# Attention and channel-mixing kernel: reordered opening, spread x loads, a shorter row stage with a Sigmoid gate, inverse-root chains cut in three

## The chip, the core and the metric

The kernel runs on one core of one Trainium2 chip. The metric is the device time of one execution in microseconds (us). An execution is also profiled: every instruction's start and duration on the five engines TensorE (PE), VectorE (DVE), ScalarE (ACT), GpSimd (POOL) and SyncE (SP, which issues DMAs).

## The reference

```python
x = x + _layernorm(_L0_attn_ref(_layernorm(x), weight))     # x: 4 x 1024 x 128
x = x + _layernorm(_L0_ffn_ref(_layernorm(x), W_r, W_k, W_v, mu_r, mu_k))
# attention, 16 heads of 8 channels, queries = keys = y, values = the whole y
scores = einsum('bhtk,bhsk->bhts', y, y) / sqrt(8)
o = einsum('bhts,bsc->bhtc', softmax(scores), y)            # then o @ weight, 2048 -> 128
# channel mixing; x_prev is x shifted by one position
r = sigmoid((mu_r * x + (1 - mu_r) * x_prev) @ W_r.T)
k = (mu_k * x + (1 - mu_k) * x_prev) @ W_k.T
out = r * (square(relu(k)) @ W_v.T)
```

## The kernel before

The work is cut into 4 batches of 1024 positions, 8 rows of 512 queries, 128 steps (row, head) and 256 quads; a quad is four key blocks of 128 against 512 queries, so a step is two quads. One loop over k runs on every engine, each engine in its own written order, with semaphores between them.

For quad k, `score(k)` writes four banks of `ps_s` on TensorE; it waits until the exponential of quad k-1 has read them. `weigh(k)` on ACT takes the exponential into `e_f` (float32). `cast(k)` on POOL issues a DMA that rounds `e_f` to the float16 `e_hi`. `split_quad` on DVE, written in iteration k+2, computes `e_lo = e_f - e_hi`. `products(k)`, written in iteration k+4 (`LAG`), multiplies y_hi by e_hi, y_hi by e_lo and y_lo by e_hi: twelve matmuls of 512 columns. After two quads `take_o` (ACT), `split_o` (DVE), `project` (TensorE), `invert` (DVE), `scale` (ACT) and `add` (DVE) normalize a head's result, apply its slice of the weight and add it to `acc`. SP loads the operands `op_s` and `op_t` four steps ahead (`OP_RING`).

When the 16 heads of row r are added, its row stage runs beside the next row's quads. `rows_at(k)` gives its offset o = k - (32 (r+1) + 8), from 0 to `SPAN` - 1, and each engine's `row_part(o, r)` says what it does at which offset: centre and statistics, an inverse root, normalize, add x, statistics, an inverse root, transpose, mix with the shifted row, key, gate and value matmuls, gating, statistics, an inverse root, normalize, add. `inv_root` (line 271) is a chain of 7 or 9 tiny POOL instructions, each waiting for the one before, in the same POOL queue as the casts. `next_batch(k)` does the same for the preparation of the next batch: statistics, root, normalize, split, squares, transposes, and a shift bound `shx` that DVE computes and TensorE transposes (`turn_shift`). The gate is computed as 1 / (1 + exp(-g)): exponential on ACT (line 569), add (781) and four reciprocals (785) on DVE. The row stage, the batch preparation and the opening share one PSUM bank, `ps_x`.

Ahead of the loop stands the opening: the first batch is loaded, normalized, split, transposed and written to DRAM scratch, the attention weight is scaled, centred (`weights_less`, `weights_centred`) and split into w_hi and w_lo. SP issues the x loads of batches 1 to 3 in one block (line 229).

## Time and profile before

| | |
|---|---|
| median of 3 runs (lowest, highest) | 1064.0 us (1063.06, 1066.88) |
| the profiled execution, its own time | 1063.41 us |
| its span, first to last instruction | 1061.6 us |
| mean granted TensorE clock | 0.954 |
| busy: PE, DVE, ACT, POOL | 88%, 85%, 69%, 28% |
| DMA engines, time of cast packets (q0) | 65.3% of the span |
| first and last exponential of the loop | 36.68 us, 996.33 us |

Busy shares are of the whole span. An engine that is idle gets the name of whatever released it; that name is the last link of a chain and need not be its cause. The granted clock is 1.0 at 2.4 GHz and 0.5 at 1.2 GHz.

### The profile page before, as it was taken

To read this page: it belongs to the slowest core of one execution; us is meant where nothing else is said; L and a number is where in the kernel's file an instruction comes from. 1 tells how busy PE (TensorE), PEld (TensorE's weight loads), DVE (VectorE), ACT (ScalarE), POOL (GpSimd) and SP (SyncE) were. 2 spreads that over 40 slices of the span, in tenths; PEclk is the share of its full clock that TensorE was granted. 3 is DMA by queue.
4 is the path that set the end of the run, shared out by engine and by line. 5 is a ranking of instruction groups with operands and counts; after the bars stand their busy time and mean duration, and the time that the engine had idled before them with its cause. 6 is when DMAs were issued, how large, how long until landed. Compare 5 with 4: busy or idle time off the path is not lost.

```text
span 1061.6 us, 17583 instructions
## 1 busy us (share of the span) xinstructions
PE 929.4 (88%) x5930; PEld 442.6 (42%) x5930; DVE 900.7 (85%) x1163; ACT 730.5 (69%) x1007; POOL 302.3 (28%) x521
## 2 busy tenths in 40 slices
PE   1659999989998899989998889988999899989922
PEld 1224444444544345434444335444444345444411
DVE  6658899889897899969988899969989689979953
ACT  1537777868777677867777667876787677777621
POOL 2101431123115541243115541153113341154021
PEclk9879999999999999989999999998999999999965
DMA  5689899998886788888987788886988788878700
GB/s 166 130 178 183 166 186 185 192 206 181 178 180 138 164 171 170 180 198 176 187 172 146 146 178 173 180 203 151 201 167 175 154 177 180 179 144 170 141 10 10
DMA packets 100344, 174.41 MB, mean 164 GB/s; under 512 B 21536, under 2 KB 62880, under 8 KB 100256
## 3 DMA queue, kind: packets, MB, share of 16 engines
q0 software_dynamic: 36864, 134.23, 65.3%
q1 hardware_dynamic: 63392, 39.06, 13.5%
q8 instruction: 48, 0.79, 0.3%
q14 instruction: 40, 0.33, 0.1%
HBM read 28.51 MB, written 10.49 MB: 37 GB/s over the span
## 4 chain that ended last, share of the span: by engine, by line
PE 37%; DVE 19%; issue 17%; POOL 13%; DMA 7%; ACT 5%; SPq 1%; DVEq 0%; POOLq 0%; ACTq 0%
PE ps_o L426 10%; POOL fnw L277 9%; PE ps_o L427 9%; PE ps_o L428 9%; DVE e_lo L703 8%; DMA e_hi<-e_f 6%; PE ps_s L411 3%; ACT e_f L524 3%; POOL nw L277 2%; POOL e_hi L314 2%; ACT part L536 2%; DVE eg L785 2%; DVE fst L730 1%; DVE o_neg L709 1%; PE ps_r L439 1%
## 5 line engine op out<-in xcount | busy, mean ns | idle before, releaser
L703 DVE TENSOR_TENSOR e_lo<-e_f,e_hi 128x2048 f16<-128x2048 f32 x256 | 590.9, 2308 | 85.9 <-DMA e_hi<-e_f 85.6
L524 ACT ACTIVATE e_f<-ps_s 128x2048 f32<-128x2048 f32 x256 | 482.0, 1883 | 181.1 <-PE ps_s L411 171.4
L426 PE MATMUL ps_o<-e_hi,y_hi 128*128 128x512 f16 x1024 | 397.4, 388 | 29.9 <-DVE o_neg L709 26.5
L428 PE MATMUL ps_o<-e_hi,y_lo 128*128 128x512 f16 x1024 | 395.3, 386 | 0.0
L427 PE MATMUL ps_o<-e_lo,y_hi 128*128 128x512 f16 x1024 | 395.2, 386 | 0.0
L314 POOL DMA_DIRECT2D e_hi<-e_f x256 | 138.2, 540 | 682.3 <-ACT e_f L524 645.7
L536 ACT ACTIVATE part<-ps_r,rden 128x128 f32<-128x128 f32 x512 | 145.8, 371 | 72.7 <-DVE rden L715 72.7
L426 PEld LDWEIGHTS ps_o<-e_hi,y_hi 128*128 128x128 f16 x1024 | 100.9, 99 | 183.6 <-issue 82.3
L428 PEld LDWEIGHTS ps_o<-e_hi,y_lo 128*128 128x128 f16 x1024 | 101.6, 99 | 125.3 <-issue 7.8
L427 PEld LDWEIGHTS ps_o<-e_lo,y_hi 128*128 128x128 f16 x1024 | 101.6, 99 | 95.1 <-issue 7.4
L411 PE MATMUL ps_s<-op_t,op_s 32*128 32x512 f16 x1024 | 102.1, 388 | 35.9 <-ACT e_f L524 25.0
L725 DVE TENSOR_TENSOR acc<-acc,part 128x512 f32<-128x512 f32 x120 | 81.6, 680 | 21.5 <-ACT part L536 21.5
L439 PE MATMUL ps_r<-w_hi,o_hi 128*128 128x128 f16 x512 | 93.0, 220 | 1.2 <-ACT part L536 1.2
L440 PE MATMUL ps_r<-w_lo,o_hi 128*128 128x128 f16 x512 | 92.9, 220 | 0.0
L441 PE MATMUL ps_r<-w_neg,o_neg 128*128 128x128 f16 x512 | 92.7, 220 | 0.0
L709 DVE SCALAR_TENSOR_TENSOR o_neg<-o_hi,ps_o 128x512 f16<-128x512 f16 x128 | 86.2, 673 | 6.9 <-ACT o_hi L529 4.8
L529 ACT ACTIVATE o_hi<-ps_o 128x512 f16<-128x512 f32 x128 | 77.7, 607 | 1.7 <-PE ps_o L428 1.7
L411 PEld LDWEIGHTS ps_s<-op_t,op_s 32*128 32x128 f16 x1024 | 26.1, 91 | 104.8 <-issue 69.4
L439 PEld LDWEIGHTS ps_r<-w_hi,o_hi 128*128 128x128 f16 x512 | 50.5, 99 | 16.9 <-issue 2.4
L440 PEld LDWEIGHTS ps_r<-w_lo,o_hi 128*128 128x128 f16 x512 | 50.4, 98 | 15.6 <-issue 1.1
L277 POOL TENSOR_TENSOR fnw<-fnw,consts 128x4 f32<-128x4 f32 x88 | 53.0, 603 | 6.9
L441 PEld LDWEIGHTS ps_r<-w_neg,o_neg 128*128 128x128 f16 x512 | 50.3, 98 | 0.0
(122 smaller groups left out, 467.1 us busy)
## 6 DMA issues: line engine op xcount, KB each, us to landing
e_hi<-e_f POOLq DMA_DIRECT2D x256, 512.0 KB, 4.9
op_t<-scr_t SPq DMA_DIRECT2D x512, 32.0 KB, 3.4
op_s<-scr_s SPq DMA_DIRECT2D x512, 16.0 KB, 3.1
scr_s<-yT SPq DMA_DIRECT2D x12, 256.0 KB, 4.5
scr_t<-yT SPq DMA_DIRECT2D x12, 256.0 KB, 3.8
xs<-in_L_attn_x_dram SPq DMA_DIRECT2D x4, 512.0 KB, 9.3
out_dram<-res SPq DMA_DIRECT2D x8, 256.0 KB, 2.2
scr_s<-eighth SPq DMA_DIRECT2D x4, 256.0 KB, 3.2
```

What stands on the lines that cost most here:

```text
L277: nc.gpsimd.tensor_tensor(out, in0, in1, op).then_inc(s, 1)
L314: nc.gpsimd.dma_start(flat(e_hi[:, ring]), flat(e_f[:, k % EF_RING])).then_inc(cast_in[ring], 16)
L411: mm = nc.tensor.matmul(ps_s[:, g, :], op_s[here, slot, q * P:(q + 1) * P], op_t[here, slot, :], start=True, stop=True)
L426: nc.tensor.matmul(dst, y_hi[:, b % 2, s, :], e_hi[:, ring, g, :], start=(q == 0 and g == 0), stop=False)
L427: nc.tensor.matmul(dst, y_hi[:, b % 2, s, :], e_lo[:, ring, g, :], start=False, stop=False)
L428: mm = nc.tensor.matmul(dst, y_lo[:, b % 2, s, :], e_hi[:, ring, g, :], start=False, stop=(q == 1 and g == 3))
L439: nc.tensor.matmul(dst, o_hi[:, j % 2, here], w_hi[:, j % H, :], start=True, stop=False)
L440: nc.tensor.matmul(dst, o_hi[:, j % 2, here], w_lo[:, j % H, :], start=False, stop=False)
L441: mm = nc.tensor.matmul(dst, o_neg[:, j % 2, here], w_neg[:, j % H, :], start=False, stop=True)
L524: nc.scalar.activation(e_f[:, k % EF_RING], ps_s[:], ACT.Exp, scale=1.0 / ROOT).then_inc(weighed, 1)
L536: ins = nc.scalar.activation(part[:, j % 2, i, :], ps_r[:, i * P:(i + 1) * P], ACT.Identity, scale=rden[:, j % 2, i:i + 1])
L703: dve.tensor_tensor(flat(e_lo[:, ring]), flat(e_f[:, k % EF_RING]), flat(e_hi[:, ring]), ALU.subtract).then_inc(split, 1)
```

## The change

**Root chains.** `inv_root` gets a part number: two steps, three steps, two or four steps. The three parts of a chain are written in three successive iterations, behind that iteration's cast. A batch's squares go from POOL to ACT.

**Row stage.** `SPAN` is 41. Offsets before and now: centre, sums, moments 3, 4, 5 to 1, 2, 3; root 7 to 4-6; normalize (ACT) 9 to 7; add x, sums, moments 11, 12, 13 to 9, 10, 11; root 15 to 12-14; z 17 to 16; transposes (PE) 19 to 17; copy (ACT) 20 to 18; mixes 22, 23 to 20, 21, the gate's first; gate matmul 26 to 22; key matmul still 24; value matmul still 28; gating 34 to 30; root 38 to 33-35; normalize 40 to 36; last add 42 to 38. The gate is a Sigmoid on ACT at offset 23, and the key matmul waits for it; add and reciprocals are gone. For the last row ACT has a Sigmoid of one column at offset 8.

**x loads.** One each at quads 6, 20 and 34, after that quad's scores.

**Opening.** The first root is computed on DVE. One Newton round of two goes from the shift bound, and `turn_shift` comes two iterations later. The maximum of w_raw and the weight's centring follow the shift on DVE, over the whole weight at once; the matmuls with `less` stand between the first four scores, and ACT and DVE split the weight a quarter per iteration. The four `op_t` loads of step 0 are issued by ACT, the four `op_s` loads by SP.

```diff
+                    sp.dma_start(*op_s_load(j, g)).then_inc(op_in[slot], 16)
+                    if j > 0:
+                        sp.dma_start(*op_t_load(j, g)).then_inc(op_in[slot], 16)
...
-            for b in range(1, B):
-                sp.dma_start(xs[:, b * NB:(b + 1) * NB, :], x_v[:, b]).then_inc(x_in[b], 16)
             for k in range(LAST):
+                if k in (6, 20, 34):
+                    b = (6, 20, 34).index(k) + 1
+                    sp.wait_ge(scored, k)
+                    sp.dma_start(xs[:, b * NB:(b + 1) * NB, :], x_v[:, b]).then_inc(x_in[b], 16)
...
+            def inv_root(part_, s, before, v, y, a, var, n, eps=consts[:, 0:1], bias=None, mean=None):
+                three_halves, minus_half, minus_one = (consts[:, i:i + 1].to_broadcast([P, n]) for i in (1, 2, 3))
+                steps = [before + (0, 2, 5)[part_]]
...
+                    pool.wait_ge(s, steps[0])
+
+                if part_ == 0:
+                    go(v, var, eps.to_broadcast([P, n]), ALU.add)
+                    go(y, v, minus_half, ALU.pow)
+                if part_ == 1:
+                    go(a, y, y, ALU.mult)
+                    go(a, a, v, ALU.mult)
+                    go(a, a, minus_half, ALU.mult)
+                if part_ == 2:
+                    go(a, a, three_halves, ALU.add)
+                    go(y, y, a, ALU.mult)
+                    if bias is not None:
+                        go(bias, mean, y, ALU.mult)
+                        go(bias, bias, minus_one, ALU.mult)
...
-                if o == 7:
-                    root_row(0, r)
-                if o == 15:
-                    root_row(1, r)
-                if o == 17:
-                    ge(pool, mix_r, r)
+                for i, first in enumerate((4, 12, 33)):
+                    if 0 <= o - first < 3:
+                        root_row(i, r, o - first)
+                if o == 14:
+                    ge(pool, mix_k, r)
...
-                if o == 38:
-                    root_row(2, r)
...
-                    if o == 20:
-                        root_batch(b)
-                    if o == 26:
-                        square_batch(b)
+                    if 19 <= o < 22:
+                        root_batch(b, o - 19)
...
+                pe.wait_ge(w_centred, 1)
...
+                    if j < 2:
+                        pe.wait_ge(w_split, j + 1)
...
-                if o == 19:
+                if o == 17:
                     pe.wait_ge(z_ok, r + 1)
...
-                if o == 24:
-                    pe.wait_ge(mix_k, r + 1)
-                    ge(pe, kv_ps, r)
-                    nc.tensor.matmul(ps_x[:], wT[:, 1, :], mix[:, 1, :], start=True, stop=True).then_inc(key_ps, 1)
-                if o == 26:
+                if o == 22:
                     pe.wait_ge(mix_r, r + 1)
-                    pe.wait_ge(key_relu, r + 1)
                     for i in range(RB):
                         mm = nc.tensor.matmul(ps_x[:, i * P:(i + 1) * P], mix[:, 0, i * P:(i + 1) * P], wT[:, 0, :],
                                               start=True, stop=True)
                     mm.then_inc(gate_ps, 1)
...
+                if o == 24:
+                    pe.wait_ge(mix_k, r + 1)
+                    pe.wait_ge(gate_ok, r + 1)
+                    nc.tensor.matmul(ps_x[:], wT[:, 1, :], mix[:, 1, :], start=True, stop=True).then_inc(key_ps, 1)
                 if o == 28:
                     pe.wait_ge(key_ok, r + 1)
-                    pe.wait_ge(gate_exp, r + 1)
...
-            weight_top()
-            pe.wait_ge(w_in, 16)
-            for i in range(3):
-                weights_less(i)
-            pe.wait_ge(w_centred, 1)
-            weights_less(3)
             for k in range(LAST):
                 if k < QUADS:
                     score(k)
+                if k == 0:
+                    weight_top()
+                if k < 4:
+                    weights_less(k)
...
+            def weights_high(i):
+                act.wait_ge(w_scale, 2)
+                act.wait_ge(w_less, i + 1)
...
+                act.wait_ge(normed, b + 1)
+                nc.scalar.activation(flat(sq[:]), flat(yn[:]), ACT.Square).then_inc(squared, 1)
...
-                if o in (9, 40):
-                    i, src, dst, done_ = (0, acc[:, r % 2], xn, a_normed) if o == 9 else (2, gated, res, f_normed)
+                if o in (7, 36):
...
-                if o == 20:
+                if o == 8 and r == ROWS - 1:
+                    nc.scalar.activation(idle[:], consts[:, 0:1], ACT.Sigmoid)
+                if o == 18:
...
+                if o == 23:
+                    act.wait_ge(gate_ps, r + 1)
+                    ge(act, f_gated, r)
+                    nc.scalar.activation(flat(gate[:]), ps_x[:], ACT.Sigmoid).then_inc(gate_ok, 1)
...
-                if o == 27:
-                    act.wait_ge(gate_ps, r + 1)
-                    ge(act, f_gated, r)
-                    nc.scalar.activation(flat(eg[:]), ps_x[:], ACT.Exp, scale=-1.0).then_inc(gate_exp, 1)
...
+            act.wait_ge(scr_in[0], 7 * 16)
+            for g in range(4):
+                act.dma_start(*op_t_load(0, g)).then_inc(op_in[0], 16)
...
+            def batch_root():
+                v, y, a = (nw[:, i, :] for i in range(3))
+                c = nr[:, 0, 0:NB]
+                step(dve.tensor_scalar(v, mv[:, :, 1], EPS, None, ALU.add))
+                step(dve.tensor_scalar(a.bitcast(I32), v.bitcast(I32), 1, None, ALU.logical_shift_right))
+                step(dve.tensor_scalar(y.bitcast(I32), a.bitcast(I32), -1.0, float(MAGIC), ALU.mult, ALU.add))
+                for _ in range(3):
+                    step(dve.scalar_tensor_tensor(out=a, in0=y, scalar=-0.5, in1=y, op0=ALU.mult, op1=ALU.mult))
+                    step(dve.tensor_tensor(c, a, v, ALU.mult))
+                    step(dve.scalar_tensor_tensor(out=y, in0=c, scalar=1.5, in1=y, op0=ALU.add, op1=ALU.mult))
+
...
+            def batch_sqrt(b):
+                v, y, a, c = (nr[:, i, :] for i in range(4))
+                step(dve.scalar_tensor_tensor(out=a, in0=y, scalar=-0.5, in1=y, op0=ALU.mult, op1=ALU.mult))
+                step(dve.tensor_tensor(c, a, v, ALU.mult))
+                step(dve.scalar_tensor_tensor(out=y, in0=c, scalar=1.5, in1=y, op0=ALU.add, op1=ALU.mult))
...
-                v, y, a, c = (nr[:, i, :] for i in range(4))
-                for _ in range(2):
-                    step(dve.scalar_tensor_tensor(out=a, in0=y, scalar=-0.5, in1=y, op0=ALU.mult, op1=ALU.mult))
-                    step(dve.tensor_tensor(c, a, v, ALU.mult))
-                    step(dve.scalar_tensor_tensor(out=y, in0=c, scalar=1.5, in1=y, op0=ALU.add, op1=ALU.mult))
...
+                dve.wait_ge(w_in, 16)
+                dve.tensor_reduce(w_max[:, 0:1], w_raw[:], AX.XY, ALU.max)
...
+                step(dve.tensor_reduce(w_mean[:], w_raw[:], AX.X, ALU.add))
+                step(dve.tensor_scalar(w_mean[:], w_mean[:], 1.0 / C, None, ALU.mult))
+                dve.tensor_tensor(w_raw[:], w_raw[:], w_mean[:].unsqueeze(2).to_broadcast([P, H, C]),
+                                  ALU.subtract).then_inc(w_centred, 1)
...
+                dve.wait_ge(w_high, i + 1)
...
-                if o == 3:
+                if o == 1:
...
-                if o == 17:
+                if o == 16:
...
-                if o == 22:
+                if o == 20:
...
-                if o == 29:
-                    dve.wait_ge(gate_exp, r + 1)
-                    dve.tensor_scalar(eg[:], eg[:], 1.0, None, ALU.add).then_inc(gate_one, 1)
-                if 30 <= o < 34:
-                    i = o - 30
-                    dve.wait_ge(gate_one, r + 1)
-                    dve.reciprocal(eg[:, i, :], eg[:, i, :]).then_inc(gate_ok, 1)
-                if o == 34:
+                if o == 30:
                     dve.wait_ge(kv_ps, r + 1)
-                    dve.wait_ge(gate_ok, RB * (r + 1))
-                    dve.tensor_tensor(flat(gated[:]), flat(eg[:]), ps_x[:], ALU.mult).then_inc(f_gated, 1)
-                if o == 35:
+                    dve.wait_ge(gate_ok, r + 1)
+                    dve.tensor_tensor(flat(gated[:]), flat(gate[:]), ps_x[:], ALU.mult).then_inc(f_gated, 1)
...
-                if o == 42:
+                if o == 38:
...
+            dve.wait_ge(moment, 1)
+            batch_root()
             batch_normalize(0, range(NB))
             batch_split(0)
+            batch_squares(0)
...
-            dve.tensor_tensor(flat(sq[:]), flat(yn[:]), flat(yn[:]), ALU.mult).then_inc(squared, 1)
-            dve.wait_ge(w_in, 16)
-            dve.tensor_reduce(w_max[:, 0:1], w_raw[:], AX.XY, ALU.max)
...
-            batch_squares(0)
```

What the edit of the row stage does to POOL's queue, at the first row's first root (`fnw` is the root's scratch, `e_hi<-e_f` a cast). Before:

```order
35 L314 DMA e_hi<-e_f 128x2048 x19
36 L277 TENSOR_TENSOR fnw<-fmv,ws 128x4
37 L277 TENSOR_TENSOR fnw<-fnw,consts 128x4
38 L277 TENSOR_TENSOR fnw<-fnw 128x4 x2
39 L277 TENSOR_TENSOR fnw<-fnw,consts 128x4 x2
40 L277 TENSOR_TENSOR fnw<-fnw 128x4
41 L277 TENSOR_TENSOR fnw<-fmv,fnw 128x4
42 L277 TENSOR_TENSOR fnw<-fnw,consts 128x4
```

POOL's queue at the same place of the changed program:

```order
33 L326 DMA e_hi<-e_f 128x2048 x16
34 L291 TENSOR_TENSOR fnw<-fmv,ws 128x4
35 L291 TENSOR_TENSOR fnw<-fnw,consts 128x4
36 L326 DMA e_hi<-e_f 128x2048
37 L291 TENSOR_TENSOR fnw<-fnw 128x4 x2
38 L291 TENSOR_TENSOR fnw<-fnw,consts 128x4
39 L326 DMA e_hi<-e_f 128x2048
40 L291 TENSOR_TENSOR fnw<-fnw,consts 128x4
41 L291 TENSOR_TENSOR fnw<-fnw 128x4
42 L291 TENSOR_TENSOR fnw<-fmv,fnw 128x4
43 L291 TENSOR_TENSOR fnw<-fnw,consts 128x4
44 L326 DMA e_hi<-e_f 128x2048
```

Nine steps in one block have become two, three and four, with a cast between.

On ACT, at the gate of the first row (`eg` is the gate's exponential, `kr` the key). Before:

```order
133 L565 ACTIVATE kr<-kr 128x512
134 L524 ACTIVATE e_f<-ps_s 128x2048
135 L536 ACTIVATE part<-ps_r,rden 128x128 x4
136 L569 ACTIVATE eg<-ps_x 128x512
137 L524 ACTIVATE e_f<-ps_s 128x2048
```

ACT at the gate of the changed program:

```order
134 L549 ACTIVATE part<-ps_r,rden 128x128 x4
135 L585 ACT_TABLE_LOAD
136 L585 ACTIVATE gate<-ps_x 128x512
137 L537 ACT_TABLE_LOAD
138 L537 ACTIVATE e_f<-ps_s 128x2048
139 L542 ACTIVATE o_hi<-ps_o 128x512
```

The compiler has put a table load ahead of the Sigmoid and another ahead of the next exponential. There are seven of the first kind (rows 0 to 6; the eighth gate needs none) and six of the second, besides the one at the program's start.

On TensorE, at the end of the opening (`ps_s<-op_t,op_s` are scores, `w_raw,less` the weight). Before:

```order
6 L387 MATMUL ps_x<-ident,shx 128x128 x8
7 L392 MATMUL ps_r<-ident,w_max 1x128
8 L394 MATMUL ps_r<-w_top,ones 128x1
9 L399 MATMUL ps_o<-w_raw,less 128x512 x2
10 L399 MATMUL ps_r<-w_raw,less 128x512
11 L399 MATMUL ps_o<-w_raw,less 128x512
12 L411 MATMUL ps_s<-op_t,op_s 128x512 x20
```

TensorE at the end of the changed opening:

```order
6 L400 MATMUL ps_x<-ident,shx 128x128 x8
7 L426 MATMUL ps_s<-op_t,op_s 128x512 x4
8 L405 MATMUL ps_r<-ident,w_max 1x128
9 L407 MATMUL ps_r<-w_top,ones 128x1
10 L415 MATMUL ps_o<-w_raw,less 128x512
11 L426 MATMUL ps_s<-op_t,op_s 128x512 x4
```

The first scores stand ahead of the weight's matmuls, which follow one per quad.

## Rows read from the trace of the kernel before

**Rows 1.** The page, part 1: busy us of each engine (share) xinstructions

```profile
PE 929.4 (88%) x5930; PEld 442.6 (42%) x5930; DVE 900.7 (85%) x1163; ACT 730.5 (69%) x1007; POOL 302.3 (28%) x521
```

**Rows 2.** Timeline of ACT, 261 to 281: start, us, engine, line, names

```profile
265.27 1.88 ACT L524 ACTIVATE e_f<-ps_s 128x2048 f32<-128x2048 f32 x1
...
270.74 1.14 ACT L536 ACTIVATE part<-ps_r,rden 128x128 f32<-128x128 f32 x4
271.99 1.88 ACT L524 ACTIVATE e_f<-ps_s 128x2048 f32<-128x2048 f32 x1
...
276.60 1.88 ACT L524 ACTIVATE e_f<-ps_s 128x2048 f32<-128x2048 f32 x1 [2.24 <-PE ps_s L411]
```

**Rows 3.** Timeline of ACT: first exponential, that of quad 8, the last

```profile
36.68 1.88 ACT L524 ACTIVATE e_f<-ps_s 128x2048 f32<-128x2048 f32 x1 [9.03 <-PE ps_s L411]
...
71.56 1.88 ACT L524 ACTIVATE e_f<-ps_s 128x2048 f32<-128x2048 f32 x1 [12.38 <-PE ps_s L411]
...
996.33 1.88 ACT L524 ACTIVATE e_f<-ps_s 128x2048 f32<-128x2048 f32 x1 [0.96 <-PE ps_s L411]
```

**Rows 4.** Waits of PE, 36.7 to 1010: us in total, times, longest

```profile
PE ps_o L426 <- DVE o_neg L709: 26.5, 19, 4.8
PE ps_s L411 <- ACT e_f L524: 25.0, 15, 3.2
PE ps_s L411 <- DMA op_t<-scr_t: 10.9, 1, 10.9
PE ps_x L387 <- DVE shx L661: 3.6, 2, 3.0
PE ps_o L426 <- DVE e_lo L703: 3.2, 2, 1.7
```

**Rows 5.** Windows, PE: window, us, busy (x), granted clock, DMA share, GB/s

```profile
157.50:996.30 838.80, 791.16 (x5130) 0.98 0.85 175
```

**Rows 6.** Timeline of POOL, 318 to 352: the third root of row 0

```profile
325.40 1.51 POOL L277 TENSOR_TENSOR fnw<-fmv,consts 128x4 f32<-128x4 f32 x1
326.99 1.03 POOL L277 TENSOR_TENSOR fnw<-fnw,consts 128x4 f32<-128x4 f32 x1
...
330.52 3.11 POOL L277 TENSOR_TENSOR fnw<-fnw,consts 128x4 f32<-128x4 f32 x2
...
334.83 0.61 POOL L314 DMA_DIRECT2D e_hi<-e_f  x1 [0.36 <-POOL fnw L277]
```

**Rows 7.** The page, parts 5 (busy, mean ns) and 6 (KB, us to landing)

```profile
L703 DVE TENSOR_TENSOR e_lo<-e_f,e_hi 128x2048 f16<-128x2048 f32 x256 | 590.9, 2308 | 85.9 <-DMA e_hi<-e_f 85.6
...
L314 POOL DMA_DIRECT2D e_hi<-e_f x256 | 138.2, 540 | 682.3 <-ACT e_f L524 645.7
...
e_hi<-e_f POOLq DMA_DIRECT2D x256, 512.0 KB, 4.9
```

**Rows 8.** Timeline of the opening

```profile
15.90 2.28 DVE L807 TENSOR_REDUCE w_max<-w_raw 128x1 f32<-128x2048 f32 x1
...
30.20 0.33 SPq L217 DMA_DIRECT2D op_s<-scr_s  x1
...
33.69 0.43 SPq L219 DMA_DIRECT2D op_t<-scr_t  x1
```

**Rows 9.** Groups by line, ACT: busy us, mean ns, idle before

```profile
L572 ACT ACT_TABLE_LOAD x1 | 1.3, 1283 | 0.7 <-PEq L862 0.7
```

**Rows 10.** The chain that ended last, from 1003: start, us, what

```profile
1018.22 0.69 DVE acc L725
...
1022.29 0.59 DVE fsum L749
...
1040.13 0.70 DVE mix L772
...
1041.66 2.09 PE ps_x L455 x2
...
1047.70 3.40 DVE eg L785 x4
```

More of the change, by code:

```diff
@@ L108, in sandwich @@
         xn = sb("xn", [P, RB, C], F32)
+        idle = sb("idle", [P, 1], F32)
         x1 = sb("x1", [P, RB, C], F32)
@@ L113, in sandwich @@
         kr = sb("kr", [P, BANK], F32)
-        eg = sb("eg", [P, RB, C], F32)
+        gate = sb("gate", [P, RB, C], F32)
         gated = sb("gated", [P, RB, C], F32)
@@ L396, in weights_less @@
             def weights_less(i):
+                pe.wait_ge(w_centred, 1)
                 if i == 2:
                     pe.wait_ge(w_scale, 1)
-                mm = nc.tensor.matmul((ps_o[:, 0, :], ps_o[:, 1, :], ps_r[:])[i % 3], less[:],
-                                      flat(w_raw[:, 4 * i:4 * i + 4, :]), start=True, stop=True)
-                mm.then_inc(w_less, 1)
+                if i == 3:
+                    pe.wait_ge(shift_ready, 1)
+                nc.tensor.matmul(weights_ps(i), less[:], flat(w_raw[:, 4 * i:4 * i + 4, :]), start=True,
+                                 stop=True).then_inc(w_less, 1)
             def score(k):
```

145 lines of the change are left out of this document (71 added, 74 removed).

## The prediction

> **What bounds the kernel now.** I read the page first: TensorE (PE) is busy 88% of the span, VectorE (DVE) 85% [rows 1]. Two engines so close to full do not say which one sets the time, so I looked for the beat of the loop. Undisturbed, a pair of quads takes 271.99 - 265.27 = 6.72 us from exponential to exponential [rows 2]. TensorE has no idle time in that beat: one score group, twelve 512-column products, and every second quad a projection. 255 intervals at 3.36 us would be 857 us. The first exponential starts at 36.68 and the last at 996.33 [rows 3], so the loop takes 959.7 us, about 102 us more than its beat. That 102 us, the 36.7 us ahead of it and the 65.2 us behind it (1061.6 - 996.33) are what a change can win.
>
> Where do the 102 us go? Next the waits of TensorE inside the loop [rows 4]: 26.5 us for o_neg, 25.0 for e_f (about 8 of them before the fifth quad, where the pipeline fills), 10.9 once for an operand DMA, 3.6 for shx, 3.2 for e_lo. Without the filling and the DMA that is 26.5 + 17 + 3.6 + 3.2 = 50 us. Then the clock: from quad 32 to the last exponential, 838.8 us, the granted clock is 0.98 of full [rows 5]; 0.02 x 838.8 = 17 us, partly inside the waits. What is left is TensorE's own work for the row stage and the batch preparation, which nothing here removes.
>
> What starts those 50 us? The engines that TensorE waits for are not the cause: DVE and ScalarE (ACT) are late because a cast is late. POOL issues the cast DMA of each quad, and the same in-order queue runs the inverse-root chains. One chain of nine small steps stood in front of a cast from 325.40 to 334.83 [rows 6]: 9.4 us between two casts that are 3.36 apart in the beat. The steps themselves are 0.2 us, the pow 1.03; the long ones (two steps in 3.11) stood still beside a running e_lo. ACT waited for the end of that chain as well, and with it the next exponential. How much delay is free? Products stand four quads behind their scores, 13.4 us. Exponential 1.88, cast issue 0.54, transfer 4.9, split 2.31 [rows 3, 7] are 9.6: some 3.8 us to spare. So a 9 us hold shows on TensorE and a 3 us hold hardly does.
>
> **The change part by part.**
>
> *Root chains in pieces.* A chain of nine steps becomes two, three and four steps with a cast behind each. By [rows 6] the first piece is 326.99 + 1.03 - 325.40 = 2.6 us, the others some 2.5 to 4 us when they meet a running e_lo subtraction. A quad has 3.36 us, less 0.54 for the cast, so each cast is late by 0 to 1.5 us, inside the margin of 3.8. Squaring a batch leaves POOL (three times) and goes to ACT, where 1024 columns take about half of the 1.88 us that 2048 take [rows 3], in a long quad: hidden. The shift is issued two quads later on TensorE, which removes the 3.6 us wait for shx. Of the 50 us I let 12 stay: two quads carry a piece of two chains at once, and ACT's two normalizations now follow the last piece by one quad. Term -38, bounds -25 (half stays) and -46. With the waits go the drops of the clock behind them: of the 17 us in [rows 5] I take -12 (bounds -5, -15).
>
> The Trainium skill (SBUF — State Buffer, terms, shared port pair) says that DVE and GpSimd lock one port pair for a whole instruction and that the loser blocks fully. The stretched steps of [rows 6] agree with it. By that rule cutting the chain shortens no step, and every piece can lose a whole subtraction: the term would be the -25 of the first rival, not -38.
>
> *x loads spread.* Three loads of x stood in one block behind the first operand loads, and TensorE waited 10.9 us for an operand [rows 4]; the exponential of quad 8 began at 71.56 [rows 3]. Now one load each is issued at quads 6, 20 and 34, each ahead of operands that are needed six quads later (20 us). That returns the 10.9 and, since TensorE comes out of such a stand at the lower clock, an estimated 2.5 more; each load still takes DMA time from the casts: +1 each. Term -10.4, bounds -4 and -13.
>
> *Opening.* The first root moves from POOL (pow 1.03 as in [rows 6] among its seven steps) to DVE (twelve short ones): an estimated -0.9. The w_max reduction (2.28 [rows 8]) and the squaring leave DVE's path, y_lo moves behind two reductions and becomes the last input: net -0.8. One Newton round fewer: -1.0. The eight operand loads of the first step were issued one by one from 30.20 to 33.69 [rows 8]; now four on SP and four on ACT's queue side by side: -1.9. First exponential about 4.6 us earlier, at 32. The weight preparation, which stood before it, now stands between the first scores on TensorE and ACT, with two full-width DVE passes over w_raw ahead of the second quad: it gives back about 2.5 by quad 8. Term -2.1, bounds +2 and -5.
>
> *Sigmoid gate.* Per row this takes an add (0.4 us) and four reciprocals (3.4 us [rows 10]) off DVE; the beat hides them now (no wait of TensorE lies there), so they count nothing in the loop except as slack. It puts a table load before the Sigmoid and another before the next exponential, six times in the loop. Before has one load only, at the very start, 1.28 us [rows 9]. In the quad concerned, the exponential follows the four scalings at once (270.74 + 1.14, then 271.99 [rows 2]). Inserting 1.28 + 0.62 + 1.28 starts it 3.1 us late, at 275.1; it ends at 277.0. TensorE has products, projection and the key matmul in that quad; the exponential after it began at 276.60 [rows 2], its score 0.45 earlier, at 276.15. So TensorE waits 0.9. I take 1.3 with hand-offs. Term +8; bounds +5 and, if nothing covers the 3.2, +19.
>
> The Trainium skill (ScalarE: Activation LUTs, What ACT_TABLE_LOAD costs) has 1.28 us for the load and a drain of about 1.38 with each switch. The row agrees on the first; no row of before shows a drain. By that figure a pair costs 2.8 us more, the wait is 3.7, and the term would be +22: this speaks against the change.
>
> *Tail.* The last sum of the last row ends at 1018.91, but its centring starts at 1022.2 [rows 10], because reciprocals, gating and statistics of row 6 stand between. With row 6 finished earlier in quads: -3.3. POOL did row 6's chain ahead of row 7's; it now starts sooner, against the DVE work of row 7, and about 1.2 less of it lies on the path: -1.3. Row 7's own gate: before, 11.0 us from mix_d (1040.13) to the end of the reciprocals (1047.70 + 3.40) [rows 10], gate exponential and add included, the value product hidden beside them. Now the order is mix_r, gate product, Sigmoid 0.6, key product 2.09 [rows 10], relu and square 1.2, value product, each product about as long as the key's: 10.1 with two mixes and hand-offs. -0.9. Term -5.5, bounds -3 and -7.
>
> *Sum* against this execution (span 1061.6, 1063.4 with what lies around it, 0.6 under the median of 1064.0): -38 - 12 - 10.4 - 2.1 + 8 - 5.5 = -60. 1063.4 - 60 = 1003.4; with the offset to the median **1004 us**.
>
> **The rivals.**
> - *The casts stay late.* The steps still stand still behind e_lo, pieces run to 4 or 5 us, and six pieces follow one another at the end of each row. For it: 3.11 us for two steps [rows 6]. Against: the margin of 3.8 us. Half of waits and clock stay: 25 + 8 us in place of 12 + 5, about +17, and 3 more for the thinner distances: 1024.
> - *Switching the table costs more than its row.* If ACT stands twice as long, each of the six is 3.6: +14, 1018.
> - *A x load stalls again* in mid-loop, where DMA is as busy as it was at quad 7. Two of three at half the old price: +11, 1015.
> - *Slower.* POOL's first piece stands one quad behind DVE's moments, where it stood two. If DVE runs late there, POOL waits for it with the next cast queued behind, DVE then waits for that cast, and the lateness feeds itself. There are 21 chains in the loop; at 60 / 21 = 2.9 us each the whole gain is gone. For it: DVE is 85% busy. Against: DVE loses 3.8 us of work per row, and in [rows 4] no wait begins at the moments. 1065 to 1080.
> - *The change does nothing:* the waits have another cause than the chains; only opening, x loads, tail and tables count: 1063 - 18 + 8 = 1053.
>
> **How the numbers follow.** Forecast 0.60 (own range 988 to 1014), casts late 0.17, table 0.10, x load 0.06, nothing 0.03, slower 0.03, the rest 0.01 about unchanged. The low end adds the favourable bounds of the two largest terms (-8, -3) and some of the opening (-5): 986. The high end takes in the late casts with a dearer table: 1030. Range 986 to 1030. A measurement of this kernel tells about 0.5% from no change, some 5 us. Faster by more: 0.95; within: 0.02; slower: 0.03.
>
> **What would show it.** First exponential near 32, that of quad 8 near 58. TensorE's waits for o_neg and e_f in the loop at about 12 us together past the filling; clock 0.99 or more there. No POOL hold above 4.5 us between casts. Seven row gates with one table load each and six loads in front of exponentials, each pair with a TensorE wait of 1 to 1.5 us behind it. From the last sum to the end 37 us in place of 42.7. Wrong if the o_neg waits stay above 15 us (pieces do not free the casts), or if the exponential behind a Sigmoid begins over 4 us late.

## The result: 1006 us, and the profile after

| | before | after |
|---|---|---|
| time, median (range), us | 1065.44 (1063.06 to 1067.48, 4 runs) | 1006.24 (1004.64 to 1009.22, 4 runs) |
| ratio to before, 95% interval | | 0.9448 (0.9413 to 0.9484) |
| profiled execution: span, us | 1061.6 | 1007.4 |
| granted clock, mean | 0.954 | 0.978 |
| first exponential, last one, end of span, us | 36.68, 996.33, 1061.6 | 31.79, 948.77, 1007.4 |

The forecast was 1004. In the two profiled executions the 54.2 us come off at three places: 4.9 ahead of the first exponential, 42.7 in the loop (959.7 to 917.0), 6.6 behind it (65.2 to 58.6). What follows in this section is the changed kernel. The page, part 1, beside [rows 1]:

```profile
PE 913.3 (91%) x5930; PEld 437.1 (43%) x5930; DVE 867.4 (86%) x1112; ACT 750.8 (75%) x1028; POOL 327.2 (32%) x513
```

Timeline of ACT, the exponentials of [rows 3]:

```profile
31.79 1.88 ACT L537 ACTIVATE e_f<-ps_s 128x2048 f32<-128x2048 f32 x1 [6.42 <-PE ps_s L426]
...
56.00 1.88 ACT L537 ACTIVATE e_f<-ps_s 128x2048 f32<-128x2048 f32 x1 [1.15 <-PE ps_s L426]
...
948.77 1.88 ACT L537 ACTIVATE e_f<-ps_s 128x2048 f32<-128x2048 f32 x1 [2.27 <-PE ps_s L426]
```

Waits of PE from 36 to 960 (total, times, longest), and the windows of the loop (busy of PE, PEld, DVE, ACT, POOL, then granted clock, DMA share, GB/s):

```profile
PE ps_s L426 <- ACT e_f L537: 16.0, 17, 2.2
PE ps_o L443 <- DVE o_neg L753: 11.2, 14, 1.4
PE ps_s L426 <- DMA op_t<-scr_t: 2.1, 1, 2.1
PE ps_x L395 <- DVE diag L683: 2.0, 2, 1.0
PE ps_x L467 <- DVE z L785: 1.3, 1, 1.3
```

```profile
31.80:138.80 107.00, 101.71 (x620) 45.12 (x620) 93.83 (x105) 81.92 (x99) 27.25 (x40) 1.00 0.95 194
138.80:948.70 809.90, 780.91 (x5138) 373.81 (x5137) 726.90 (x890) 643.60 (x879) 285.56 (x418) 1.00 0.89 182
```

The reader is to see three things. The 10.9 us DMA wait of [rows 4] has become 2.1. The o_neg wait is less than half, its longest case 1.4 in place of 4.8. But o_neg and e_f together are still 27 us, spread over 31 waits of about 1 us. Of these, 1.9 us are the filling of the pipeline (8.1 before), so 25 us stand against the 12 that were predicted, and 29 with diag and z. The granted clock is 1.00 in both windows, where [rows 5] had 0.98.

Why 25 are left shows on POOL. Row 0's third root, that of [rows 6], now ends at 298.33, and the first root of row 1 follows in the next quads. Timeline of POOL, this first root of row 1, between two casts each time:

```profile
298.69 0.58 POOL L326 DMA_DIRECT2D e_hi<-e_f  x1 [0.36 <-POOL fnw L291]
299.29 2.27 POOL L291 TENSOR_TENSOR fnw<-fmv,ws 128x4 f32<-128x4 f32 x1
301.64 1.04 POOL L291 TENSOR_TENSOR fnw<-fnw,consts 128x4 f32<-128x4 f32 x1
302.97 0.62 POOL L326 DMA_DIRECT2D e_hi<-e_f  x1 [0.30 <-POOL fnw L291]
303.62 2.78 POOL L291 TENSOR_TENSOR fnw<-fnw 128x4 f32<-128x4 f32 x2
306.47 0.20 POOL L291 TENSOR_TENSOR fnw<-fnw,consts 128x4 f32<-128x4 f32 x1
307.03 0.57 POOL L326 DMA_DIRECT2D e_hi<-e_f  x1 [0.36 <-POOL fnw L291]
307.62 2.20 POOL L291 TENSOR_TENSOR fnw<-fnw,consts 128x4 f32<-128x4 f32 x1
...
311.45 0.57 POOL L326 DMA_DIRECT2D e_hi<-e_f  x1 [0.36 <-POOL fnw L291]
```

Timeline of DVE beside it:

```profile
299.21 2.29 DVE L747 TENSOR_TENSOR e_lo<-e_f,e_hi 128x2048 f16<-128x2048 f32 x1 [0.53 <-DMA e_hi<-e_f]
...
303.44 2.29 DVE L747 TENSOR_TENSOR e_lo<-e_f,e_hi 128x2048 f16<-128x2048 f32 x1
...
307.48 2.29 DVE L747 TENSOR_TENSOR e_lo<-e_f,e_hi 128x2048 f16<-128x2048 f32 x1
```

Casts now start 4.3, 4.1 and 4.4 us apart, against a beat of 3.36. Each piece holds one step that began just behind an e_lo subtraction and ended just behind it: 2.27 us from 299.29, ending 0.06 after the subtraction; two steps in 2.78; 2.20. Such steps are 0.2 us otherwise. The three intervals lose 0.9, 0.7 and 1.1 us, and at the end of a row six pieces follow one another (here the third root's last interval, 294.39 to 298.69, was 4.3 as well).

A piece can also meet two subtractions. Timeline of POOL, second piece of row 0's second root; the same 5.7 us stand at 451.70 and 690.17:

```profile
216.04 0.61 POOL L326 DMA_DIRECT2D e_hi<-e_f  x1 [0.30 <-POOL fnw L291]
216.68 2.55 POOL L291 TENSOR_TENSOR fnw<-fnw 128x4 f32<-128x4 f32 x2
219.31 2.12 POOL L291 TENSOR_TENSOR fnw<-fnw,consts 128x4 f32<-128x4 f32 x1
221.73 0.57 POOL L326 DMA_DIRECT2D e_hi<-e_f  x1 [0.30 <-POOL fnw L291]
```

Where a piece of the batch's root and one of a row's stand in one quad, POOL is away from the casts from 565.27 to 571.93, 6.7 us, the longest case.

The same lateness reaches ACT, which waits for the last step of a root in front of its normalization (timeline of ACT):

```profile
298.37 1.65 ACT L573 ACTIVATE res<-gated,fnw 128x128 f32<-128x128 f32 x4 [1.00 <-POOL fnw L291]
```

A gate's quad on ACT, and the score that waits behind it on PE:

```profile
250.72 1.13 ACT L549 ACTIVATE part<-ps_r,rden 128x128 f32<-128x128 f32 x4
251.87 1.28 ACT L585 ACT_TABLE_LOAD   x1
253.16 0.60 ACT L585 ACTIVATE gate<-ps_x 128x512 f32<-128x512 f32 x1
253.78 1.28 ACT L537 ACT_TABLE_LOAD   x1
255.07 1.88 ACT L537 ACTIVATE e_f<-ps_s 128x2048 f32<-128x2048 f32 x1
```

```profile
257.01 0.39 PE L426 MATMUL ps_s<-op_t,op_s 32*128 32x512 f16 x4 [0.81 <-ACT e_f L537]
```

The exponential starts 4.35 us after the four scalings began, as worked out from [rows 2] (270.74 to 275.1); the rows join within 0.02 us, so there is no further stand at a switch. TensorE loses 0.81, the same behind five of the gates.

### The profile page after: what moved, and what is told of

It reads as the page before. It is cut to its first block, busy times and chain, and to the rows that moved or that the text cites. A ratio compares the mean times of both kernels' runs of the same rounds, so it can differ in the third digit from the quotient of the medians.

```text
span 1007.4 us, 17595 instructions
## 1 busy us (share of the span) xinstructions
PE 913.3 (91%) x5930; PEld 437.1 (43%) x5930; DVE 867.4 (86%) x1112; ACT 750.8 (75%) x1028; POOL 327.2 (32%) x513
## 4 chain that ended last, share of the span: by engine, by line
PE 54%; POOL 12%; DVE 10%; issue 8%; ACT 8%; DMA 4%; SPq 3%; POOLq 0%; DVEq 0%; ACTq 0%
PE ps_o L443 14%; PE ps_o L445 13%; PE ps_o L444 13%; POOL fnw L291 9%; PE ps_s L426 5%; ACT e_f L537 5%; DVE e_lo L747 4%; DMA e_hi<-e_f 3%; PE ps_r L458 2%; PE ps_r L457 2%; PE ps_r L456 2%; POOL e_hi L326 2%; POOL nw L291 1%; SPq L232 1%; SPq L230 1%
## 5 line engine op out<-in xcount | busy, mean ns | idle before, releaser
L747 DVE TENSOR_TENSOR e_lo<-e_f,e_hi 128x2048 f16<-128x2048 f32 x256 | 584.3, 2282 | 53.3 <-DMA e_hi<-e_f 52.4
L443 PE MATMUL ps_o<-e_hi,y_hi 128*128 128x512 f16 x1024 | 391.9, 383 | 11.4 <-DVE o_neg L753 11.2
L445 PE MATMUL ps_o<-e_hi,y_lo 128*128 128x512 f16 x1024 | 389.5, 380 | 0.0
L444 PE MATMUL ps_o<-e_lo,y_hi 128*128 128x512 f16 x1024 | 389.4, 380 | 0.0
L326 POOL DMA_DIRECT2D e_hi<-e_f x256 | 140.5, 549 | 609.2 <-ACT e_f L537 546.6
L291 POOL TENSOR_TENSOR fnw<-fnw,consts 128x4 f32<-128x4 f32 x88 | 81.5, 926 | 5.8
L426 PEld LDWEIGHTS ps_s<-op_t,op_s 32*128 32x128 f16 x1024 | 26.3, 91 | 96.7 <-issue 58.6
```

The lines of the kernel that those rows point to most:

```text
L291: nc.gpsimd.tensor_tensor(out, in0, in1, op).then_inc(s, 1)
L326: nc.gpsimd.dma_start(flat(e_hi[:, ring]), flat(e_f[:, k % EF_RING])).then_inc(cast_in[ring], 16)
L426: mm = nc.tensor.matmul(ps_s[:, g, :], op_s[here, slot, q * P:(q + 1) * P], op_t[here, slot, :], start=True, stop=True)
L443: nc.tensor.matmul(dst, y_hi[:, b % 2, s, :], e_hi[:, ring, g, :], start=(q == 0 and g == 0), stop=False)
L444: nc.tensor.matmul(dst, y_hi[:, b % 2, s, :], e_lo[:, ring, g, :], start=False, stop=False)
L445: mm = nc.tensor.matmul(dst, y_lo[:, b % 2, s, :], e_hi[:, ring, g, :], start=False, stop=(q == 1 and g == 3))
```

## The experiments

Twelve kernels, in three sets on the chip, each set beside runs of the kernel before; the ratios are to those (medians 1070.3, 1064.9 and 1065.5 us). The changed kernel's own 0.9448 was measured apart, with an interval of 0.35% either way, so differences of under some 5 us between it and another are not told apart by the times alone. "Loop" is from the first to the last exponential of the profiled execution: 959.7 before, 917.0 after. One profiled execution can lie some us off its median: that of the changed kernel took 1009.22 us, 3 above, those of experiments 3 and 5 are 4 below theirs (979.86 and 997.01), so a difference of loops says less than its digits.

### 1. Whole chains in the changed kernel

```diff
-                for i, first in enumerate((4, 12, 33)):
-                    if 0 <= o - first < 3:
-                        root_row(i, r, o - first)
+                if o in (5, 13, 34):
+                    root_row((5, 13, 34).index(o), r, 0)
...
-                    if 19 <= o < 22:
-                        root_batch(b, o - 19)
+                    if o == 20:
+                        root_batch(b, 0)
```

(a call with part 0 issues all the steps)

> The changed kernel with every root chain issued whole again, between two casts. Theory 1 (cutting the chains is what took TensorE's waits for o_neg and e_f down from 51.5 to 27.2 us): the chains hold the casts for 9 to 12 us again, these two waits come back to 45 to 55 us in sum, and the time is 1026 to 1036 us. Rival (the waits fell because the gate's reciprocals left VectorE and the rows' work moved to other quads; the cut is worth little): the waits stay under 35 us and the time is within 6 us of the changed kernel's 1006.

Measured: 1045.65 us, ratio 0.9777 (0.9726 to 0.9827), about 35 us more than the changed kernel; loop 957.5. Its waits of PE:

```profile
PE ps_s L426 <- ACT e_f L537: 23.5, 22, 2.6
PE ps_o L443 <- DVE o_neg L753: 17.4, 20, 2.0
PE ps_x L467 <- DVE z L785: 13.4, 7, 3.3
PE ps_x L395 <- DVE diag L683: 4.2, 3, 1.5
PE ps_o L443 <- DVE e_lo L747: 3.4, 3, 1.7
```

The expected two waits reach 40.9, not 45 to 55, and the time is above the expected 1026 to 1036: a part of the price stands behind z. Three of its waits, 3.0 to 3.3 us, are in rows 1, 3 and 5, where this edit puts the batch's whole chain and a row's second one into successive quads (337.84 to 349.92 in the trace); in the kernel before they start three quads apart. So this run is somewhat harder on the casts than the old chains were. In all five rows 61.9 against the 30.5 of the changed kernel's rows for the same names: +31. The rival (cut worth little) is out. The loop grew by 40.5, so some 9 us more came with the waits; the granted clock is 0.97 in the first 107 us and 0.99 behind them.

### 2. The cut alone, in the kernel before

```diff
-                if o == 7:
-                    root_row(0, r)
-                if o == 15:
-                    root_row(1, r)
-                if o == 38:
-                    root_row(2, r)
+                for i, first in enumerate((6, 14, 37)):
+                    if 0 <= o - first < 3:
+                        root_row(i, r, o - first)
```

(the batch's chain likewise, at 19 to 21)

> The kernel before with its root chains cut into three pieces between casts and nothing else changed. Theory 1 (the cut takes the waits): o_neg and e_f in sum fall from 51.5 us to 25 to 30, the loop loses 22 to 27 us, the time is 1037 to 1043. If the granted clock of the loop, 0.98 before, rises with it because TensorE stands still less, up to 12 us more: 1025 to 1031. Rival (the cut alone does little): 1055 to 1062. A third case: without the removal of the reciprocals the pieces collide with VectorE's longer row work and the waits stay near 45 us, 1055.

Measured: 1032.14 us, ratio 0.965 (0.9618 to 0.9682), 37 us less than before; loop 928.5, 31 less. Waits of PE:

```profile
PE ps_s L411 <- ACT e_f L524: 22.6, 14, 2.9
PE ps_s L411 <- DMA op_t<-scr_t: 13.0, 2, 10.2
PE ps_x L387 <- DVE shx L661: 7.7, 3, 2.9
PE ps_o L426 <- DVE o_neg L709: 4.2, 8, 1.4
```

o_neg and e_f fall to 26.8 as expected (shx grows from 3.6 to 7.7), and the granted clock behind the opening rises to 0.99:

```profile
157.50:964.20 806.70, 778.29 (x5100) 371.90 (x5099) 746.60 (x923) 624.17 (x863) 277.06 (x419) 0.99 0.88 181
```

At these offsets a row's last chain and the next row's first share two quads, and five intervals between casts are 6.1 to 6.3 us; the waits fall all the same. Both directions agree: cutting the chains is worth 35 to 37 us by the ratios, waits and clock together, out of 59 (31 and 40 by the loops).

### 3. What the chains still cost

Five of the steps, the Newton round behind the power, are left out of every root on GpSimd, so the last digits of the normalizations differ:

```diff
-                if part_ == 1:
-                    go(a, y, y, ALU.mult)
-                    go(a, a, v, ALU.mult)
-                    go(a, a, minus_half, ALU.mult)
                 if part_ == 2:
-                    go(a, a, three_halves, ALU.add)
-                    go(y, y, a, ALU.mult)
```

> The changed kernel with the five Newton steps left out of every root on GpSimd (the power operation's own result is used, so the normalizations' last digits differ): a chain is two steps, and two more for the bias. What the chains still cost the changed kernel in all. Theory (pieces of 3.5 to 3.9 us are a whole beat long, the casts run late behind them, and the 11 us of o_neg waits and the 8 us behind ScalarE's normalizations are of that): the two waits fall from 27 to under 12 us, the time by 12 to 18 us, to 988 to 994. Rival (the o_neg waits come from VectorE's own batch and row work, and only the normalizations' waits go): 998 to 1000. Rival (neither): 1005.

Measured: 984.05 us, ratio 0.9242 (0.9215 to 0.9269), 22 us less than the changed kernel, more than the theory's 12 to 18; loop 893.0, 24 less; the stretch behind it 5.5 less. Waits of PE, and POOL between two casts:

```profile
PE ps_s L420 <- ACT e_f L531: 7.3, 10, 1.0
PE ps_o L437 <- DVE o_neg L747: 6.5, 10, 1.1
```

```profile
294.81 0.63 POOL L291 TENSOR_TENSOR fnw<-fmv,ws 128x4 f32<-128x4 f32 x1
...
297.98 0.62 POOL L320 DMA_DIRECT2D e_hi<-e_f  x1 [1.42 <-ACT e_f L531]
```

POOL is idle 1.4 us ahead of the cast and waits for ACT, no longer for its own chain. The two waits are 13.8 us, almost the 12 of the prediction (the theory had under 12): that number described a kernel whose pieces mostly fit the beat. The 22 us are not the price of the late casts alone: behind the loop, where there are no casts, the shorter chains save on the path itself.

### 4. The batch's root apart from the row's

```diff
-                    if 19 <= o < 22:
-                        root_batch(b, o - 19)
+                    if 23 <= o < 26:
+                        root_batch(b, o - 23)
```

(normalization to 26 and 27, square to 29, split to 30, rest to 31)

> The changed kernel with the batch's root chain four quads later, so that its three pieces no longer stand in the same quads as pieces of a row's second chain; the batch's normalization, square, split and rest move with it. Theory (two pieces between one pair of casts hold the casts 6.7 us, three times a run, and the o_neg waits of 1.0 to 1.4 us that follow are of that): 3 to 6 us less, 1001 us, and no step of 6 us or more between casts. Rival (the waits there come from VectorE's own batch work, normalization and split, which only moves): within 1.5 us of 1006.

Measured: 1007.09 us, ratio 0.9458 (0.9429 to 0.9487); o_neg 10.7, e_f 19.5. The theory falls: no interval with two chains is left, and the o_neg waits stay, so the 6.7 us hold was not what they hung on. Alone, the coincidence costs nothing that shows. The rival (the waits come from VectorE's own batch work) fits the time but is not shown.

### 5. ACT's normalizations one quad later

```diff
-                if o in (7, 36):
-                    i, src, dst, done_ = (0, acc[:, r % 2], xn, a_normed) if o == 7 else (2, gated, res, f_normed)
+                if o in (8, 37):
+                    i, src, dst, done_ = (0, acc[:, r % 2], xn, a_normed) if o == 8 else (2, gated, res, f_normed)
```

> The changed kernel with ScalarE's two row normalizations one quad later (quads 8 and 37 of the row instead of 7 and 36), so that the root's last piece is done before ScalarE comes to them. Theory (ScalarE stands 1.0 to 2.2 us at the head of these quads for the last piece, and TensorE 0.6 to 2.2 us behind it for e_f): the 8 or so gaps, 8 us in sum, go, and the time is 998 to 1002. Rival (slack elsewhere is less than it looks, the quads that lose a gap get another behind): 1004 to 1007. Rival that it gets worse: x1's addition at quad 9 or the residual's at 38 now stands for ScalarE, VectorE waits 1 us and more, and the time is 1010.

Measured: 1001.33 us, ratio 0.9398 (0.9371 to 0.9425); loop 904.8. Waits of PE:

```profile
PE ps_o L443 <- DVE o_neg L753: 12.8, 12, 2.3
PE ps_s L426 <- ACT e_f L537: 6.6, 11, 0.8
```

e_f falls by 9.4 us, o_neg rises by 1.6, the time falls by 5, at the edge of what the times tell apart: by the waits, the distance of one quad between last piece and normalization was too short.

### 6. The gate: Tanh, the old gate, a second pair of loads

Three kernels. A Tanh, for which ACT loads no other table in the loop (the 1 is added in VectorE's product, the half folded into the weights; here and with the old gate the one-column Sigmoid of the last row is left out as well):

```diff
-                    nc.scalar.activation(flat(gate[:]), ps_x[:], ACT.Sigmoid).then_inc(gate_ok, 1)
+                    nc.scalar.activation(flat(gate[:]), ps_x[:], ACT.Tanh, scale=0.5).then_inc(gate_ok, 1)
...
-                    dve.tensor_tensor(flat(gated[:]), flat(gate[:]), ps_x[:], ALU.mult).then_inc(f_gated, 1)
+                    dve.scalar_tensor_tensor(out=flat(gated[:]), in0=flat(gate[:]), scalar=1.0, in1=ps_x[:],
+                                             op0=ALU.add, op1=ALU.mult).then_inc(f_gated, 1)
```

The old gate:

```diff
-                    nc.scalar.activation(flat(gate[:]), ps_x[:], ACT.Sigmoid).then_inc(gate_ok, 1)
+                    nc.scalar.activation(flat(gate[:]), ps_x[:], ACT.Exp, scale=-1.0).then_inc(gate_exp, 1)
...
+                    dve.tensor_scalar(gate[:], gate[:], 1.0, None, ALU.add).then_inc(gate_one, 1)
...
+                    dve.reciprocal(gate[:, i, :], gate[:, i, :]).then_inc(gate_ok, 1)
```

The second pair:

```diff
-                if o == 8 and r == ROWS - 1:
+                if (o == 8 and r == ROWS - 1) or (o == 13 and r < ROWS - 1):
                     nc.scalar.activation(idle[:], consts[:, 0:1], ACT.Sigmoid)
```

> The changed kernel with the gate as a Tanh instead of a Sigmoid (sigmoid(g) = (1 + tanh(g/2)) / 2: the 1 is added in VectorE's multiplication, the half is folded into the weights once), so that ScalarE loads no other table in the loop. Theory 1 (a pair of table loads costs TensorE the 0.81 us that stand behind it in the trace): 5 to 7 us less, 1000 us. Rival (ScalarE has slack and the 0.81 us are given back within some quads): within 2 us of 1006. Rival (each switch drains and costs 2.6 us that only show as a later wait): 15 us less or more, 990.

> The changed kernel with the gate of before at the new places: an Exp of the negated sum on ScalarE at quad 23 of the row, the addition of 1 at quad 24 and four reciprocals at quads 25 to 28 on VectorE, no table load in the loop. Theory (the Sigmoid trades VectorE's 0.9 to 4 us per row quad for 0.81 us of TensorE per row and comes out about even or a little ahead): within 6 us of the changed kernel, 1000 to 1012 us, with o_neg waits up by 5 to 12 us and the 0.81 us gaps gone. Rival 1 (VectorE's freed time is what makes the quads without waits possible, so it carries much of the 24 us fall of the waits): 1018 us or more. Rival 2 (the table loads cost more than the page of waits shows): 996 us or less.

> The changed kernel with one more pair of table loads per row (a Sigmoid on one column at the start of quad 13 of the row, 6 more pairs). Theory 1 (a pair costs TensorE about 0.8 us, all of it on the path): 4 to 9 us more, 1012. Rival (hidden in ScalarE's slack): within 2 us. Rival (load and drain at each switch, 5.3 us a pair, of which 3.7 reach TensorE): 22 us more, 1028.

Measured: Tanh 1004.68 us beside 1070.3 of before, ratio 0.9395 (0.9356 to 0.9433); old gate 1001.82, 0.9407 (0.9375 to 0.9438); second pair 1017.55, 0.9514 (0.9477 to 0.9552). So by the point values the table loads cost about 6 us, and the Sigmoid is some 4 us slower than the exponential, addition and four reciprocals that it replaced; the intervals of both kernels overlap that of the changed kernel. With the Tanh the waits of 0.81 us behind the gates are gone, but the e_f waits are 15.9 us in all, as before, since others, of up to 1.8 us, have come up. Freeing VectorE brought the loop nothing: with the old gate o_neg is 6.6 us, less than with the Sigmoid (11.2) where the theory had 5 to 12 more, and rival 1 falls.

The second pair (it came to seven, not six: rows 0 to 6). Timeline of ACT, and waits of PE:

```profile
215.85 1.28 ACT L577 ACT_TABLE_LOAD   x1
...
217.35 1.28 ACT L537 ACT_TABLE_LOAD   x1
218.64 1.88 ACT L537 ACTIVATE e_f<-ps_s 128x2048 f32<-128x2048 f32 x1
```

```profile
PE ps_s L426 <- ACT e_f L537: 30.5, 26, 2.2
PE ps_o L443 <- DVE o_neg L753: 7.1, 7, 2.0
```

e_f waits grow by 14.5 us, 2.1 a pair, o_neg waits shrink by 4.1; the loop is 7.1 longer, 1.0 a pair. A pair's price on TensorE depends on the quad (0.81 in the gate's; 2.0 three times and 1.3 three times here), and part of it is a wait that would have come anyway. The 22 us of a drain are out: 7 us more were measured, by the ratios as by the loops.

### 7. The x loads in one block again

```diff
             for j in range(OP_RING):
                 load(j)
+            for b in range(1, B):
+                sp.dma_start(xs[:, b * NB:(b + 1) * NB, :], x_v[:, b]).then_inc(x_in[b], 16)
...
-                if k in (6, 20, 34):
-                    b = (6, 20, 34).index(k) + 1
-                    sp.wait_ge(scored, k)
-                    sp.dma_start(xs[:, b * NB:(b + 1) * NB, :], x_v[:, b]).then_inc(x_in[b], 16)
```

> The changed kernel with its three x loads in one block ahead of the loop again, as before the change. Theory (the block costs TensorE the 10.4 us of one wait for op_t, as taken in the prediction, and in the changed kernel a wait of 2.1 us is left): 7 to 10 us more, 1014 to 1016, one wait of some 10 us for op_t near 45 to 60 us. If the granted clock of the opening, 0.90 before between 36.7 and 157.5 us and 1.00 after, fell because of that stop, the clock of the first 120 us is 0.9 again and the time is 1020 to 1028. Rival (the opening in its new order gives the operand loads a start ahead of the block): within 2 us of 1006, clock 1.00.

Measured: 1020.39 us, ratio 0.9579 (0.9554 to 0.9605), 14 us more than the changed kernel where the theory had 7 to 10 (11 more by the loops). Waits of PE, the exponential of quad 8, and windows of PE in and behind the wait (busy, then granted clock):

```profile
PE ps_s L424 <- DMA op_t<-scr_t: 12.2, 1, 12.2
```

```profile
68.64 1.88 ACT L535 ACTIVATE e_f<-ps_s 128x2048 f32<-128x2048 f32 x1 [13.60 <-PE ps_s L424]
```

```profile
62.00:68.00 6.00, 0.02 (x4) 0.50 0.92 190
68.00:71.00 3.00, 3.00 (x10) 0.50 0.22 50
```

The exponential of quad 8 is 12.6 us later (68.64 against 56.00), all but 0.4 of it the one wait; the changed kernel has its own wait of 2.1 us later, at 77.90, so over the loop the wait carries 10.1. The clock of the first 107 us is 0.95, in the changed kernel 1.00. Most of that costs nothing: it fell to the lower level while TensorE stood still, and only some 3 us of work behind the wait ran at it, about 1.5 us lost. The e_f waits are 4 us longer than in the changed kernel (20.0); the rest is not told apart. With the block in both, quad 8 is at 71.56 before and 68.64 here, so the new opening is worth 2.9 us by then (4.8 at the first exponential).

### 8. The first step's op_t loads on SyncE

```diff
-                    if j > 0:
-                        sp.dma_start(*op_t_load(j, g)).then_inc(op_in[slot], 16)
+                    sp.dma_start(*op_t_load(j, g)).then_inc(op_in[slot], 16)
...
-            act.wait_ge(scr_in[0], 7 * 16)
-            for g in range(4):
-                act.dma_start(*op_t_load(0, g)).then_inc(op_in[0], 16)
```

> The changed kernel with the first step's four op_t loads back in SyncE's queue behind the op_s loads. Theory (the two queues issue side by side, which was taken as 1.9 us): the first exponential at 33.5 to 34 us instead of 31.8, the time 1.5 to 2 us longer. Rival (the four loads share the engines of the DMA queues and land as late either way): the first exponential within 0.3 us of 31.8 and the same time.

Measured: 1008.26 us, ratio 0.9474 (0.9444 to 0.9503): the interval takes in no difference. The place in the trace is clear, 1.58 us later than in the changed kernel:

```profile
33.37 1.88 ACT L536 ACTIVATE e_f<-ps_s 128x2048 f32<-128x2048 f32 x1 [8.24 <-PE ps_s L425]
```

### 9. The pieces put together

Tanh, later normalizations and the batch's root apart; then the same without the last.

> The changed kernel with the Tanh gate, the batch's roots apart and the normalizations one quad later together. Theory (the three remove different waits: 6, 4 and 6 us): 990 us, e_f waits under 6 us in sum. Rival (they share the same slack, and the time saved at one place is lost at the next): 998 to 1001.

> The changed kernel with the Tanh gate and the normalizations one quad later, the batch's roots left where the change has them. The batch's roots moved alone changed nothing (ratio 0.9458 to before, against 0.9448 of the changed kernel); Tanh alone gave 0.9395 and the later normalizations alone 0.9398. Theory (the two remove different waits and add up, the roots' place is worth nothing): ratio 0.934 to 0.936, 994 to 996 us, as with all three. Rival (in the kernel with all three the roots' place paid for a part): 0.938, 999 us, or the o_neg waits of 2 us and more that stood in the kernel with all three come from the moved roots and the ratio is 0.931, 991.

Measured: all three 994.95 us, ratio 0.934 (0.9312 to 0.9368); without the batch's move 998.58, 0.9388 (0.9364 to 0.9413). The first is 1.1% faster than the changed kernel, with intervals apart. e_f waits are down to 3.0 and 2.6 us, o_neg waits up to 19.7 and 19.5 in the two. The second kernel misses its theory (0.934 to 0.936) and fits the rival by which the root's place paid for a part. But the batch's root was worth nothing alone, and the 5 us between these two are not explained: the waits are the same and the intervals touch. It stays open.

## Why the prediction was right, term by term

| term | predicted | measured | by |
|---|---|---|---|
| root chains: waits, past the filling | -38 | -22 to -31 | waits of PE, experiments 2, 1 |
| root chains: waits and clock | -50 | -35 to -37 | medians, experiments 1, 2 |
| x loads spread | -10.4 | -14 (-11 by the loops) | experiment 7 |
| opening | -2.1 | -2.9 | quad 8, block in both |
| gate, table loads | +8 | +4 to +6, not clear of noise | experiment 6 |
| behind the loop | -5.5 | -6.6 | spans |
| sum (without the first line) | -60 | -53 to -57 | |
| the kernel | -60 | -54 profiled, -59 by medians | |

The mechanism was right: casts queued behind chains that held POOL 9 us. The size of the first term was not. The step that failed is "each cast is late by 0 to 1.5 us, inside the margin of 3.8". Many delays are indeed about 1 us, but in the run of pieces shown the next quad gives none of it back: three pieces add up to 2.7 us, six pieces follow one another at the end of a row, and the normalization one quad behind the last piece waits for it. The prediction had named this last place, and the quads with two chains, and let 12 us stay for both. Of the waits that were to fall from 50 to 12, 25 to 29 us stayed. That chains cause the larger part is shown by experiment 3 (13.8 left where the pieces are shorter), and that a good part of them hung on the normalization's place by experiment 5. The largest piece was mis-sized too: "some 2.5 to 4 us" for a piece came to 4.8 where it met two subtractions (216.68 to 221.43), so "no POOL hold above 4.5" failed with a single chain, at 5.7 us between casts, as well as where two met, at 6.7; the latter cost nothing alone (experiment 4). It is the first rival's price for the waits (25 left), while the clock, of which that rival let 8 us stay, went up to 1.00 all the same. So -50 was 13 to 15 too much, the other terms together gave 8 to 9 more than taken (x loads 3.6, gate 2 to 4, tail 1.1, opening 0.8). The forecast lies 6 us under the profiled execution and 2 under the median because these offset: that nearness is luck, the main mechanism is not. The low end of the range is a slip: 1004 less 8, 3 and 5 is 988, not 986.

The 2.5 us that the prediction put on the clock behind the x loads' wait has a row: in the kernel before the clock is 0.50 from 72 to 76 us, after TensorE restarted at 70.89. That a load of x costs 1 us of the casts' DMA time is an estimate that no run here isolates.

What the trace showed was that a step that meets an e_lo stands until its end, and cutting shortened none. From 90 to 960 us the mean step of a chain took 0.83 us with the chains whole (experiment 1) and 0.87 in the changed kernel; 0.65 in the kernel before and 0.78 with the cut alone (experiment 2). Cutting won by letting the casts through, not by less standing. The rule of the Trainium skill (SBUF — State Buffer, terms, shared port pair), that the loser of the port pair blocks for a whole instruction, agrees with these rows. The -25 that the prediction gave as its outcome is what the waits did (-22 to -31); where it and my reading of the margin differed, the rule had the size.

At a switch of tables the rows join within 0.02 us, at the gate and at the extra pairs; a gate costs TensorE 0.81 us, where the prediction worked out 0.9 and took 1.3. The Trainium skill (ScalarE: Activation LUTs, What ACT_TABLE_LOAD costs) and these rows agree on the load of 1.28 us; the drain of about 1.38 that it adds to each switch shows in no row here, and the measurement decides.

The tail, from the last sum's end to the end, is 1007.4 - 969.96 = 37.4 us, predicted 37; the first exponential 31.8, predicted 32; quad 8 at 56.0, predicted 58. A wait of 2.1 us for an operand is left at 77.90. The first x load, placed behind quad 6's scores, left SP's queue only at 64.90, 13 us ahead of it; that it causes the wait is not shown. It would be the rival "a x load stalls again" at a fifth of its price.

## What to carry to other kernels

Work that shares an in-order queue with a periodic DMA issue has to be cut so that a piece and the issue fit one period at the length that the steps have beside the busiest neighbour, not at their own: experiment 2 shows what cutting alone is worth (37 us), and 3 what shorter chains are worth on top (22 us, some of it behind the loop). Slack is a sum over consecutive periods: three pieces of +0.9 are one delay of 2.7. And before an engine that is 85% busy is relieved at the price of one that is 69% busy, ask which of the two the critical engine waits for in that quad: at the gate it was the second.

## What the runs showed of the hardware

- The granted clock followed TensorE's stops: with the chains whole 0.97 and 0.99 in the two windows, with them cut 1.00 and 1.00. In experiment 7 it was 1.00 up to 60 us, 0.50 from 62 to 71, while TensorE stood from 55.8 to 67.98 and for 3 us of work behind it, and 1.00 from 72. In experiment 1 the loop grew by 9 us more than the waits did.
- A small step on GpSimd (128x4: an addition or multiplication 0.20 us alone, the power 1.03) that began beside a running e_lo subtraction ended just behind it: 2.27 us in the rows above, up to 3.04 for the power, 3.19 in experiment 2. The subtraction itself took 2.29 in all three. In the changed kernel the steps with constants average 0.93 us (0.60 before), and POOL is busier (327.2 us) than before (302.3) with eight instructions fewer.
